# Router matmuls before the key projection, and the keys' low part behind the second row maximum

## What is computed

```python
x = x + tanh(g_xattn) * xattn(layernorm(x), ctx, ctx)          # q, k, v, softmax, output projection
n = layernorm(x)
logits = n @ Wr + br                                           # the router, 8 columns
top_vals, top_idx = top_k(logits, 2); gate = softmax(over the two)
h = relu(einsum('td,edh->teh', n, W1) + b1)
y = einsum('teh,ehd->ted', h, W2) + b2
x = x + tanh(g_ffn) * einsum('ted,te->td', y, gate)
```

## Time and profile before

| | |
|---|---|
| median of 3 runs | 823.16 us (821.69 to 823.32) |
| the profiled execution | 824.68 us |
| its span, first to last instruction | 822.9 us |
| granted TensorE clock, mean over the span | 0.968 |
| first phase: starts of the first and the last row maximum | 24.3 and 376.4 us of the span |
| PE busy | 726.2 us, 88% |
| DVE busy | 606.9 us, 74% |
| POOL busy | 458.7 us, 56% |
| ACT busy | 406.1 us, 49% |

### The profile page before, as it was taken

How to read it: one execution, slowest core, us unless ns; L and a number is a source line. 1 busy time by engine, 2 the same in 40 slices (tenths; PEclk the granted TensorE clock), 3 DMA queues, 4 the chain that set the end, 5 groups by cost and what they waited for, 6 DMA issues and landing times.

```text
span 822.9 us, 21358 instructions
## 1 busy us (share of the span) xinstructions
PE 726.2 (88%) x6536; PEld 486.8 (59%) x6537; DVE 606.9 (74%) x1256; ACT 406.1 (49%) x783; POOL 458.7 (56%) x453
## 2 busy tenths in 40 slices
PE   3688889888888888878899999999999999999982
PEld 2345555454444544534577777777777777777761
DVE  5767898888888898897466787667766666676653
ACT  3266777676766776657343233333333333333340
POOL 6224554566566665437657678654665555556522
PEclk9799999999999999977899999999999999999997
DMA  6446656676756666653233233442323332333321
GB/s 187 133 119 201 189 151 197 141 194 167 185 143 182 188 161 173 153 145 117 54 91 53 46 53 46 55 53 40 53 45 47 46 48 45 50 51 52 44 31 20
DMA packets 96789, 85.32 MB, mean 104 GB/s; under 512 B 22256, under 2 KB 86000, under 8 KB 96592
## 3 DMA queue, kind: packets, MB, share of 16 engines
q1 hardware_dynamic: 80752, 65.73, 29.4%
q0 software_dynamic: 15680, 18.69, 14.5%
q10 hardware_dynamic: 288, 0.00, 0.0%
HBM read 53.61 MB, written 30.62 MB: 102 GB/s over the span
## 4 chain that ended last, share of the span: by engine, by line
PE 49%; DVE 18%; issue 14%; DMA 8%; ACT 4%; POOL 4%; POOLq 1%; another core or an unknown queue 1%; DVEq 0%; ACTq 0%; SPq 0%
PE banks L1794 15%; DVE negmax L1137 7%; DMA out_dram<-yb,dest_idx 6%; PE banks L1776 5%; PE banks L1778 5%; PE banks L1777 5%; PE banks L1688 4%; PE banks L1598 3%; ACT probs L946 2%; PE banks L1676 2%; PE banks L1731 2%; POOL xg L716 2%; PE banks L1584 2%; DVE stats L1061 2%; PE banks L1762 1%
## 5 line engine op out<-in xcount | busy, mean ns | idle before, releaser
L1009 ACT ACTIVATE hid<-banks,b_col 128x256 f32<-128x256 f32 (+1 forms) x312 | 124.1, 452 | 213.3 <-DVE hl L1479 101.1
L1794 PE MATMUL banks<-wall,hh 128*128 x568 | 204.8, 380 | 1.4 <-DVE hl L1479 1.0
L793 POOL DMA_INDIRECT out_dram<-yb,dest_idx x71 | 125.2, 1764 | 127.1 <-DMA out_dram<-yb,dest_idx 54.7
L1137 DVE TENSOR_REDUCE negmax<-banks 128x4 f32<-128x1024 f32 x128 | 155.5, 1217 | 21.7 <-PE banks L1648 20.3
L1776 PE MATMUL banks<-xh,wall 128*128 128x256 f16 (+1 forms) x624 | 162.6, 265 | 6.9 <-ACT hid L1009 3.6
L946 ACT ACTIVATE probs<-banks 128x1024 f32<-128x1024 f32 x128 | 131.0, 1024 | 66.5 <-PE banks L1676 63.0
L1777 PE MATMUL banks<-xl,wall 128*128 128x256 f16 (+1 forms) x624 | 162.4, 265 | 0.0
L1778 PE MATMUL banks<-xh,wall 128*128 128x256 f16 (+1 forms) x624 | 162.4, 264 | 0.0
L1794 PE MATMUL banks<-wall,hl 128*128 x568 | 144.3, 273 | 0.0
L1688 PE MATMUL banks<-probs,vaug 128*32 128x256 f32 x1024 | 84.2, 401 | 24.1 <-ACT probs L946 15.0
L701 POOL DMA_INDIRECT token_lists<-entry,place_i x64 | 70.5, 1102 | 61.7 <-ACT probs L946 40.9
(11 more groups left out here) (203 smaller groups left out, 1177.3 us busy)
## 6 DMA issues: line engine op xcount, KB each, us to landing
raw<-in_L_ffn_W SPq DMA_DIRECT2D x16, 512.0 KB, 5.1
wst<-in_L_ffn_W SPq DMA_DIRECT2D x16, 512.0 KB
k_parts<-kparts SPq DMA_DIRECT2D x48, 128.0 KB
q_parts<-qparts SPq DMA_DIRECT2D x48, 128.0 KB
ks<-k_parts SPq DMA_DIRECT2D x64, 96.0 KB, 2.3
qs<-q_parts SPq DMA_DIRECT2D x64, 96.0 KB
xin<-in_x SPq DMA_DIRECT2D x16, 256.0 KB, 2.9
cin<-in_ctx SPq DMA_DIRECT2D x16, 256.0 KB, 3.1
```

Source lines behind the costliest of these rows:

```text
L793: nc.gpsimd.indirect_dma_start(out_rows, bass.IndirectOffsetOnAxis(dest_idx[par][:, s:s + 1], 0), yb[par][:, s, :], None, compute_op=ALU.a ...
L1009: ins = nc.scalar.activation(hid[half][:, c % (HC // 2), 0:subs(j) * P], banks[:, b, c % 2 * TS:c % 2 * TS + subs(j) * P], ACT.Relu, bias= ...
L1137: nc.vector.tensor_reduce(negmax[:, c, 8 * (g // 2):8 * (g // 2) + 8].rearrange("p (m g p2) -> p m g p2", m=2, g=2)[:, :, g % 2, :], banks ...
L1794: ins = nc.tensor.matmul(dst, h_[:, c, s * P:(s + 1) * P], w_, start=(c == 0 and k == 0), stop=(c == HC - 1 and k == 1))
```

## The change

TensorE issues `router` before `k` in step 0, and VectorE does `k_low` after `reduce` 1 instead of before it. Nothing is added or taken away.

```diff
 # VectorE, body, loop over w
                     if gating and w == 0:
                         places(q)
-                    if w == 1 and ahead:
-                        k_low(m + 1)
                     if w == 3 and post:
                         attended_low(m - 2)
                     if maxima:
                         reduce(m, w)
+                    if w == 1 and ahead:
+                        k_low(m + 1)
                     if w == 7 and turns:
                         norm_low(m + 2)
 # TensorE, body, u == 0
                         if attention:
                             turn_max(m - 1, 1)
+                        if judged:
+                            router(m - 3, t - 2 if lists_at(m, par, LEAD + 1) else None)
                         if ahead and not first_batch:
                             k(m + 1, 1 - par, 0)
                             k(m + 1, 1 - par, 1)
-                        if judged:
-                            router(m - 3, t - 2 if lists_at(m, par, LEAD + 1) else None)
```

## The result

The changed kernel took 837.0 us in the median (834.13 to 838.52), against 822.75 us for the kernel before beside it: a ratio of 1.0161 [1.0135, 1.0187], slower by 14.3 us. The forecast was 831.5 us within 826.0 to 835.7. The sign was right, the size too small, and the range missed.

What follows compares the result with a forecast made beforehand. TensorE bounds a body up to the second maximum, then VectorE. 6.32 (eight bodies) + 0.50 (12, 13) + 0.25 (2) + 1.23 (0) = 8.3 us slower: 831.5 us median, 8-in-10 range 826.0 to 835.7.

Steps and rivals of the forecast that it cites:

- What bounds a body: Each body: TensorE sets the time up to the second maximum, VectorE from there on, 93.67 of 96.88 us busy.
- the list of signs: Trace signs, e.g. `logits` 1.3 us sooner except bodies 8 and 10, low part 1.14 to 1.23 us after the maximum's start.
- The wait for `logits`: VectorE's 17.9 us idle before `logits`, in 11 places; `logits` some 1.3 us earlier was to bring no gain by itself.
- The catch-up at the end of a body: Rival: steps 6 and 7 absorb the delay, leaving body 0's 1.2 us, 824.4 us; chance 0.10 (partial catch-up 0.05).
- The router moved up at no price: TensorE, router ahead of keys: their sum stays, second maximum no earlier, no cost; doubt 0.01 us a body.
- 0.79 us in line: VectorE, low part behind the second maximum: costs 0.79 us a body, less what that maximum gains; upper bound 0.87 us.
- Bodies 12, 13, 2 and 1: Bodies 12, 13 and 2: maximum gains 0.54 us, VectorE pays 0.25 us each; body 1: nothing taken.
- Bodies 8 and 10: Lap-starting bodies: `logits` stays late, maximum starts 0.79 us earlier, low part follows; nothing lost or won.
- its rival: Bodies 8 and 10: if the router were the wait, maximum 1.30 us earlier, 0.51 us won each, sum 7.3 us; no chance given.
- Body 0: 1.23 us: Body 0: query projection waits for the low part, so the chain grows by one maximum, 1.23 us, uncovered.
- the first of the sum: Bodies 3, 4, 5, 6, 7, 9, 11, 14: second maximum gains nothing, each pays 0.79 us, 6.32 us together.
- the 12.5 us of the upper bound: Whole kernel: thirteen bodies at 0.87 us and body 0, 12.5 us slower, or 835.7 us.

Runs made afterwards that it cites:

- the low part alone: Kernel before with only the keys' low part moved behind the second maximum, router left behind the key projection: 834.58 us, ratio 1.0107.
- The router alone: Kernel before with only the router moved ahead of the key projection, keys' low part left ahead of the second maximum: 833.01 us, ratio 1.0094.
- The second's 11.0 us: The changed kernel measured and profiled once more, unaltered, beside the kernel before: 835.58 us, ratio 1.0132.
- The edit that freed `share` in the changed kernel: GpSimd's bias addition (L665) put ahead of the list entry L701: 829.54 us on the changed kernel, 823.05 us on the kernel before.

## Why the prediction was right in its sign and wrong in its size

- **What bounds a body: right.** The second maximum still starts with its scores (226.20 by the chain, 226.22 in body 9), the low part follows it by 1.14 us, and VectorE stands idle 2.14 us ahead of it, as the list of signs had it. The wait for `logits` bought nothing. The catch-up at the end of a body did not come: bodies 3, 4 and 5 keep 0.72 to 0.80 us.
- **The router moved up at no price: right** with the low part behind the maximum (the low part alone gives the same bodies). The router alone showed what lay under it: keys that come later cost some 0.6 us as soon as something stands behind them.
- **0.79 us in line: right.** The step from the second to the third maximum gave 0.78 to 0.80 us in every body from 3 to 14.
- **Bodies 12, 13, 2 and 1:** +0.14, +0.37, +0.25, +0.20 against 0.25, 0.25, 0.25, 0. In body 12 that is luck: its second maximum came 0.22 us earlier instead of 0.54, and the hold of `onehot` that fell away, 0.54 us, made up for it.
- **Bodies 8 and 10:** -0.09 and -0.46 against 0, by a reading that failed. The prediction took the late start as a delay that stays in front of `logits`, and its list of signs excepted these two bodies. It did not stay. Body 8 in the changed kernel:

```profile
198.41 0.96 PE L1731 MATMUL banks<-wr,x2T 128*128 128x8 f32 x8
...
201.42 0.38 PE L1648 MATMUL banks<-ks,qs 48*128 48x256 f16 x4
...
199.41 0.17 DVE L1129 TENSOR_TENSOR logits<-banks,br_b 128x16 f32<-128x16 f32 x1
...
202.29 1.22 DVE L1137 TENSOR_REDUCE negmax<-banks 128x4 f32<-128x1024 f32 x1 [2.49 <-PE banks L1648]
```

`logits` starts 0.04 us behind the router's end instead of 1.35, and what is left is 0.49 us between the end of the scores and the second maximum. So that maximum came 0.87 us earlier (0.99 in body 10), between the 0.79 of the reading and the 1.30 of its rival, and the low part took 0.79 of it. Bodies 12 and 13, which are no laps, had `logits` 0.60 and 0.64 us behind the router's end, and lost that too. No run shows that the lap is its cause; where it comes from is open.

- **Body 0: 1.23 us.** 1.12 us up to the query projection. The whole body paid 1.62 us in the first profile of the changed kernel, with the hold of `wo`, and 0.58 in the second, without it.
- **The step that failed** is the first of the sum: "Bodies 3, 4, 5, 6, 7, 9, 11, 14: the maximum starts within 0.05 us of its scores already, so it gains nothing. 8 x 0.79 = 6.32 us". It took the delay through the body unchanged, and its upper bound was the low part's own 0.87 us a body. I asked which engine waits for VectorE and looked at TensorE, ScalarE and SyncE; I did not lay VectorE's delayed instructions beside GpSimd's timetable. What happened there is 1.46 us more in bodies 9 and 11, and also in 7, where a gap of 0.95 us before the fourth maximum closed at the same time; and 0.8 us less in 6 and 14. The eight bodies measured 0.72 + 0.80 + 0.80 + 0.01 + 1.22 + 2.28 + 2.26 + 0.04 = 8.13 us, against 6.32.
- **What misled it** is the earlier trace rows: 93.67 us "busy" of 96.88. In that sum 1.19 us of body 6 and 1.60 us of body 14 are `onehot`, an instruction of some 0.2 us: waits written as work. Some 2.4 us of it was slack, which could take in a delay, and took in 1.6.
- **Beyond the bodies** the prediction had no term: 1.8 us of the difference of the profiles lie ahead of the first maximum and behind the last. Behind it, code that no edit touches took 444.2 to 448.9 us over the profiles of these kernels, so differences of a few us there are not the change's. So the failed step is not the whole miss. The first comparison's 14.3 us are 6.0 above the forecast: 2.0 lie in the bodies (1.8 of them in the eight), 1.8 outside them, and 2.1 are the distances of the two profiled executions from their medians. The second's 11.0 us are 2.7 above it and inside the 12.5 us of the upper bound. Whether the first comparison's 14.3 us or the second's 11.0 is nearer is open, and so is the cause of the closed gap in body 7, which the view of waits puts down to "remote" in the kernel before.

## What to carry to other kernels

Before delaying work on VectorE, lay its next small SBUF instructions beside GpSimd's timetable: a shift of 0.8 us moved one of 0.16 us into a hold of 1.5 us, and moved others out of theirs. A group whose mean is far above its shortest member (363 ns against 160) is a wait that the view of waits cannot show, so a stretch is not full because its engine reads busy there. And a wait at the head of a view is worth something only if what stands behind it could then start sooner; here 17.9 us of it could be taken away without any gain.

## What was not expected of the hardware

- A 128x4 VectorE instruction is recorded as busy for up to 1.78 us, ten times its 0.16 us, while GpSimd adds two SBUF tensors; it ends within 0.1 us of that addition.
- GpSimd's indirect DMA instruction (L701) holds it as well, to its end (0.27 to 0.28 us instead of 0.16 in bodies 7, 9 and 11, where the addition was out of the way), and the addition behind it follows without letting VectorE in between: `share` started 0.30 us ahead of the addition and lost.
- The edit that freed `share` in the changed kernel moved a hold onto another instruction in the kernel before (`chosen`, 1.70 us): the hold is a property of the two timetables, so each shift has to be looked at in both kinds of bodies.
